# Modulation sections 3 to 6 weighted on VectorE and computed later in the V pass

## The reference, cut to what matters

```python
mod = (_silu(L0_c) @ L0_wmod).reshape(L0_c.shape[0], 6, 1, -1)
sa, ca, ga, sb, cb, gb = (mod[:, 0], mod[:, 1], mod[:, 2], mod[:, 3], mod[:, 4], mod[:, 5])
ga = (2 * (ga >= 0) - 1) * jnp.maximum(jnp.abs(ga), 0.25)
gb = (2 * (gb >= 0) - 1) * jnp.maximum(jnp.abs(gb), 0.25)
h = _layernorm(x, axis=-1) * (1 + ca) + sa
x = x + ga * _L0_attn_ref(h, L0_attn_W_K, L0_attn_W_Q, L0_attn_W_V, L0_attn_W_O)
h = _layernorm(x, axis=-1) * (1 + cb) + sb
x = x + gb * _L0_ffn_ref(h, ...)
```

## Time and profile before

| | us |
|---|---|
| median of 3 runs | 2128.99 (2128.67 to 2129.42) |
| profiled execution, its own time | 2128.4 |
| its span (first to last instruction) | 2126.6 |
| TensorE busy | 2077.6 (98%) |
| VectorE busy | 1352.4 (64%) |
| ScalarE busy | 1029.5 (48%) |
| GpSimd busy | 712.6 (34%) |

### The profile page before, as it was taken

The page is one execution under the profiler, slowest core; times in us unless marked ns, Lnnn a source line. Parts: engine busy times, 40 slices in busy tenths (PEclk is TensorE's granted clock), DMA queues, the critical chain, the costliest instruction groups (busy, mean ns, idle before and its releaser), DMA issues. The chain is left out here.

```text
span 2126.6 us, 36789 instructions
## 1 busy us (share of the span) xinstructions
PE 2077.6 (98%) x12049; PEld 1811.6 (85%) x12049; DVE 1352.4 (64%) x3065; ACT 1029.5 (48%) x1947; POOL 712.6 (34%) x539
## 2 busy tenths in 40 slices
PE   7999899999999999999999999999998999999898
PEld 5778698999999999999999999999997888788687
DVE  7422366675766756656667565565654778799865
ACT  4322355555555545555555555555553333688511
POOL 3310143261442524524336000000026444588300
PEclk9999999999999999999999999999998999999999
DMA  7666312212122121221221201201034666101121
GB/s 266 199 208 188 122 50 63 74 53 77 42 76 67 57 62 42 77 67 57 62 62 57 68 23 52 62 22 52 25 111 145 221 222 231 60 31 40 55 69 60
DMA packets 171419, 189.99 MB, mean 89 GB/s; under 512 B 13395, under 2 KB 119123, under 8 KB 171219
## 3 DMA queue, kind: packets, MB, share of 16 engines
q1 hardware_dynamic: 169043, 184.89, 27.8%
q10 hardware_dynamic: 2304, 4.20, 0.5%
HBM read 121.53 MB, written 67.50 MB: 89 GB/s over the span
## 5 line engine op out<-in xcount | busy, mean ns | idle before, releaser
L1056 ACT ACTIVATE pT_hi<-ps_t 128x512 fp32r<-128x512 f32 (+3 forms) x640 | 304.2, 535 | 250.3 <-PE ps_t L994 248.2
L1137 DVE TENSOR_TENSOR pT_lo<-ps_t,pT_hi 128x512 fp32r<-128x512 f32 (+3 forms) x640 | 356.1, 604 | 62.8 <-ACT pT_hi L1056 62.3
L1064 ACT ACTIVATE probs<-probs,rmin 128x128 f32<-128x128 f32 (+15 forms) x256 | 309.2, 1209 | 161.5 <-DVE rmin L1128 161.0
L193 PE MATMUL ps_z<-pT_lo,v_hi 128*128 128x256 f32 (+1 forms) x1152 | 325.7, 283 | 0.0
L194 PE MATMUL ps_z<-pT_hi,v_lo 128*128 128x256 f32 (+1 forms) x1152 | 325.4, 282 | 0.0
L192 PE MATMUL ps_z<-pT_hi,v_hi 128*128 128x256 f32 (+1 forms) x1152 | 318.4, 276 | 0.3 <-DVE pT_lo L1137 0.3
L994 PE MATMUL ps_t<-ident,probs 128*128 128x128 f32 x2176 | 285.5, 274 | 2.8 <-ACT probs L1064 2.8
L994 PEld LDWEIGHTS ps_t<-ident,probs 128*128 128x128 f32 x2176 | 246.2, 141 | 11.8 <-ACT probs L1064 3.1
L192 PE MATMUL ps_s<-kT_hi,qT_hi 128*128 128x512 f32 (+3 forms) x640 | 248.3, 388 | 1.3 <-DVE qT_lo L1104 1.1
L194 PE MATMUL ps_s<-kT_hi,qT_lo 128*128 128x512 f32 (+3 forms) x640 | 233.4, 365 | 0.0
L193 PE MATMUL ps_s<-kT_lo,qT_hi 128*128 128x512 f32 (+3 forms) x640 | 232.7, 364 | 0.0
(11 more groups left out here) (148 smaller groups left out, 4113.8 us busy)
## 6 DMA issues: line engine op xcount, KB each, us to landing
scratch_v<-p_vo_hi SPq DMA_DIRECT2D x64, 256.0 KB, 2.6
scratch_v<-p_vo_lo SPq DMA_DIRECT2D x64, 256.0 KB, 3.3
v_hi<-scratch_v SPq DMA_DIRECT2D x64, 256.0 KB, 3.4
v_lo<-scratch_v SPq DMA_DIRECT2D x64, 256.0 KB, 3.7
scratch_zT<-z SPq DMA_DIRECT2D x256, 64.0 KB, 1.7
w_raw<-in_w_qkv SPq DMA_DIRECT2D x16, 512.0 KB, 3.7
o_z<-scratch_zT SPq DMA_DIRECT2D x16, 512.0 KB, 6.0
o_scales<-scratch_recips SPq DMA_DIRECT2D x16, 512.0 KB, 7.3
```

Of the source, the lines that this page charges most:

```text
L193: nc.tensor.matmul(dst, stat[0], mov[1], start=False, stop=False)
L1056: nc.scalar.activation(pT[0][:, slot, i % 2, 0:w], ps_t[:, (chunks_before(i) + u) % T_BANKS, 0:w], ACT.Copy).then_inc(t_hi, 1)
L1064: nc.scalar.activation(probs[:, i % 2, 0:w], probs[:, i % 2, 0:w], ACT.Exp, bias=rmin[:, i % 2:i % 2 + 1], scale=-1.0, accum_out=sums[:, i ...
L1137: nc.vector.tensor_tensor(pT[1][:, slot, i % 2, 0:w], ps_t[:, (chunks_before(i) + u) % T_BANKS, 0:w], pT[0][:, slot, i % 2, 0:w].bitcast(F ...
```

## The change

For sections 2 to 5, VectorE now multiplies each of the four chunks of `w_mod` by its 128 values of `silu(c)`, one per partition, and adds the four up in a buffer of 128 x 512 (`summed`, which is the second half of `absr`): one `tensor_scalar` and three `scalar_tensor_tensor` per section (`add_chunk`, the letter K). TensorE then adds over the partitions with one fp32 matmul against `ones`, in place of four. Sections 0 and 1 stay as they were.

The four sections are moved: on TensorE from before V4, V8, V12 and V14 to before V20, V27, V34 and V41. The uses G2 to G5 move behind X20, X27, X34 and X41 on VectorE. On SyncE's queue the loads of sections 2 to 5 move from in front of O0, O0, O4 and O8 to in front of O4, O10, O18 and O25. A load into a half of `wm` now waits for the last K that read it.

```diff
+    summed = absr[:, 1, :]
...
+    part_step = sem("part_step")
...
-    PE_FIRST = """M0 M1 T0.0 T0.1 T0.2 T0.3 V0 V1 T1.0 T1.1 T1.2 T1.3 V2 V3 M2 V4 V5 T2.0 T2.1 T2.2 T2.3 V6 V7 M3 V8 V9
-        T3.0 T3.1 T3.2 T3.3 V10 V11 M4 V12 V13 M5 V14 V15"""
+    PE_FIRST = """M0 M1 T0.0 T0.1 T0.2 T0.3 V0 V1 T1.0 T1.1 T1.2 T1.3 V2 V3 V4 V5 T2.0 T2.1 T2.2 T2.3 V6 V7 V8 V9 T3.0
...
-    V_FIRST = NT
+    V_FIRST = 44
...
-                if s >= 2:
+                if 2 <= s < 4:
                     sp.wait_ge(mod_ready, s - 1)
+                elif s >= 4:
+                    sp.wait_ge(part_step, DC * (s - 3))
...
-            if n == V_FIRST + 6:
-                load("v3")
...
+        def add_chunk(s, c):
+
+            chunk, scale = wm[:, s % 2, c, :], c_silu[:, c:c + 1]
+            if c == 0:
+                dve.wait_ge(wm_loaded[s], 16)
+                dve.wait_ge(mod_used, s)
+                ins = nc.vector.tensor_scalar(summed, chunk, scale, None, ALU.mult)
+            else:
+                dve.wait_ge(part_step, DC * (s - 2) + c)
+                ins = nc.vector.scalar_tensor_tensor(out=summed, in0=chunk, scalar=scale, in1=summed,
+                                                     op0=ALU.mult, op1=ALU.add)
+            ins.then_inc(part_step, 1)
...
             if s >= 2:
                 pe.wait_ge(mod_used, s - 1)
-            pe.wait_ge(wm_loaded[s], 16)
-            for c in range(DC):
-                last = nc.tensor.matmul(ps_mod[:, s % 2, :], c_wide[:, c, :], wm[:, s % 2, c, :],
-                                        start=(c == 0), stop=(c == DC - 1))
+                pe.wait_ge(part_step, DC * (s - 1))
+                last = nc.tensor.matmul(ps_mod[:, s % 2, :], ones[:, :], summed, start=True, stop=True)
+            else:
+                pe.wait_ge(wm_loaded[s], 16)
+                for c in range(DC):
+                    last = nc.tensor.matmul(ps_mod[:, s % 2, :], c_wide[:, c, :], wm[:, s % 2, c, :],
+                                            start=(c == 0), stop=(c == DC - 1))
             last.then_inc(mod_ready, 1)
```

More of the change, by code:

```diff
@@ L398, in prologue @@
     rows_kept = {2: gate_a, 5: gate_b}
-    PE_FIRST = """M0 M1 T0.0 T0.1 T0.2 T0.3 V0 V1 T1.0 T1.1 T1.2 T1.3 V2 V3 M2 V4 V5 T2.0 T2.1 T2.2 T2.3 V6 V7 M3 V8 V9
-        T3.0 T3.1 T3.2 T3.3 V10 V11 M4 V12 V13 M5 V14 V15"""
[L405 to L408, removed]
+    PE_FIRST = """M0 M1 T0.0 T0.1 T0.2 T0.3 V0 V1 T1.0 T1.1 T1.2 T1.3 V2 V3 V4 V5 T2.0 T2.1 T2.2 T2.3 V6 V7 V8 V9 T3.0
+        T3.1 T3.2 T3.3 V10 V11 V12 V13 V14 V15 V16 V17 V18 V19 M2 V20 V21 V22 V23 V24 V25 V26 M3 V27 V28 V29 V30 V31
+        V32 V33 M4 V34 V35 V36 V37 V38 V39 V40 M5 V41 V42 V43"""
+    ACT_FIRST = """D0 H0 H1 H2 H3 A0.0 A0.1 A0.2 D1 A0.3 Y0 Y1 A1.0 A1.1 A1.2 D2 A1.3 Y2 Y3 Y4 D3 Y5 A2.0 A2.1 A2.2
+        A2.3 Y6 Y7 Y8 Y9 A3.0 A3.1 A3.2 A3.3 Y10 Y11 Y12 Y13 Y14 Y15 Y16 Y17 Y18 Y19 Y20 Y21 Y22 Y23 Y24 Y25 Y26 Y27
+        Y28 Y29 Y30 Y31 Y32 Y33 Y34 Y35 Y36 Y37 Y38 Y39 Y40 Y41 Y42 Y43"""
+    DVE_FIRST = """S0 G0 N0 G1 S1 L0.0 L0.1 L0.2 L0.3 N1 X0 X1 S2 L1.0 L1.1 X2 N2 X3 S3 X4 X5 L2.0 L2.1 N3 X6 X7 X8 X9
+        L3.0 L3.1 X10 X11 X12 X13 X14 K2.0 X15 K2.1 X16 K2.2 X17 K2.3 X18 X19 X20 G2 X21 K3.0 X22 K3.1 X23 K3.2 X24
+        K3.3 X25 X26 X27 G3 X28 K4.0 X29 K4.1 X30 K4.2 X31 K4.3 X32 X33 X34 G4 X35 K5.0 X36 K5.1 X37 K5.2 X38 K5.3 X39
+        X40 X41 G5 X42 X43"""
     POOL_FIRST = """I0 I1 I2 I3 L1.2 L1.3 J1.0 J1.1 J1.2 J1.3 L2.2 L2.3 L3.2 L3.3 WK WQ"""
-    SP_FIRST = """Rc Rm0 Rx0 Rm1 Rv0 Rx1 Rx2 Rx3 Rm2 Rm3 Rv1 O0 O1 O2 O3 Rm4 O4 O5 Rv2 Rw O6 O7 Rm5 O8 O9 O10 O11 O12 O13
-        O14 O15"""
-    V_FIRST = NT
+    SP_FIRST = """Rc Rm0 Rx0 Rm1 Rv0 Rx1 Rx2 Rx3 Rv1 O0 O1 O2 O3 Rm2 O4 O5 Rv2 Rw O6 O7 O8 O9 Rm3 O10 O11 O12 O13 O14
+        O15 O16 O17 Rm4 O18 O19 O20 O21 Rv3 O22 O23 O24 Rm5 O25 O26 O27 O28 O29 O30 O31 O32 O33 O34 O35 O36 O37 O38
+        O39 O40 O41 O42 O43"""
+    V_FIRST = 44
     def entries(text):
@@ L633, in _ @@
         for what, arg in entries(DVE_FIRST):
-            {"S": statistics, "G": use_section, "N": normalise, "L": low, "X": value_lo}[what](*numbers(arg))
+            {"S": statistics, "G": use_section, "N": normalise, "L": low, "X": value_lo, "K": add_chunk}[what](*numbers(arg))
         for n in range(V_FIRST, NV):
```

## The result

The changed kernel takes 2130.57 us (median of 22 runs, 2128.45 to 2132.86), the kernel before on the same chip 2128.21 (22 runs). The ratio is 1.0015, with a 95% interval from 1.0009 to 1.0021: slower by 2.4 us by the medians and 3.2 by the ratio, some 0.15%, and outside the predicted range of 2122.1 to 2127.9. The forecast was a gain of 4.1.

What follows compares the result with a forecast made beforehand. TensorE bounds the V pass after V14; before, VectorE, ScalarE and stores run close behind. Terms: 10.3 + 1.9 - 6.5 (new waits) - 1.6 = 4.1 us less, from 2128.99 to 2124.9; range 2122.1 to 2127.9.

Steps and rivals of the forecast that it cites:

- TensorE's work, 10.3 less: Modulation matmuls of four sections: 13.7 us before, 3.4 after, so 10.3 us less on TensorE.
- V5 2.4 late by X3: Before V5, TensorE waits 2.4 us for X3, which stands behind N2 on VectorE.
- the old wait before V6 gone: Before V6, X4 now ends in time, so the earlier wait of 1.9 us disappears.
- V8 1.7 late: Before V8, TensorE waits 1.7 us, since N3 ends at 55.0 and X6 at 55.6.
- V9 1.0 and V12 1.9: Waits of 1.0 us before V9 and 1.9 before V12, with stores O5 and O7 landing late.
- The clock stays up: In TensorE's new gaps before V steps, the sum counted no loss from a lower clock.
- The rival with 0.07: TensorE's clock falls in the new gaps, 2.4 us a step; falls at V5, V8 and V12 give 2132.1; chance 0.07.
- The late loads, 1.6: Loads of sections 4 and 5 behind O17 and O24 make X late and cost 1.6 us.
- The upper bound of 2.6: Both new loads cost 2.6 us if each costs the 1.3 seen at V's last load.
- The jam rival (0.12): Loads behind O17, O21 and O24 overfill the queue by 2.1 us; gain 1.3, time 2127.7; chance 0.12.
- The ring order: On the DMA queue, a load issued behind a store should not delay it; waits 4.6, gain about 6 us.
- K free, VectorE's room: Sixteen K fit into VectorE's 2.06 us of idleness before an X, even at 1.52 each; no cost.

Runs made afterwards that it cites:

- Kernel 8: Changed kernel with the loads of sections 2 and 3 back at their places before the first stores; 2126.9 us, ratio 0.9995.
- kernel 14: Kernel 12 with two matmuls that nobody reads before V5 and one before V8; 2120.41 us, ratio 0.9964.
- kernel 13: Changed kernel with two matmuls that nobody reads before V5 and four before V8; 2130.5 us, ratio 1.0012.
- kernel 3: Changed kernel without VectorE's sixteen K; TensorE's single matmul reads a block of x in place of `summed`; 2130.49 us, ratio 1.0012.
- kernel 6: Changed kernel with the loads of sections 4 and 5 in 256 KB pieces, one behind each of O15 to O18 and O24 to O27; 2125.91 us, ratio 0.9988.
- Kernel 1: Changed kernel without the loads of sections 4 and 5, whose K read what lies in the buffer; 2127.47 us, ratio 0.9998.
- kernel 5: Kernel before with one more 1 MB load that nobody needs, behind O17; 2130.54 us, ratio 1.0009.
- kernel 4: Kernel before with two more 1 MB loads that nobody needs, behind O17 and O24; 2134.5 us, ratio 1.0031.
- kernel 12: Changed kernel with sections 2 and 3 loaded early, sections 4 and 5 and V's last load in pieces, section 5's behind O26 to O29; 2119.62 us, ratio 0.9959.
- Kernel 11: Changed kernel with the loads of sections 2 and 3 before the first stores and those of 4 and 5 in pieces; 2123.35 us, ratio 0.9979.
- kernel 7: Changed kernel, but sections 2 and 3 on four matmuls before V5 and V8, 4 and 5 by K before V18 and V26, loads as before; 2123.1 us.
- kernel 9: Kernel before with V's last load cut into four 256 KB pieces behind O21 to O24; 2126.22 us, ratio 0.9993.
- kernel 2: Changed kernel with two matmuls that nobody reads before V5 and two before V8; 2130.9 us, ratio 1.0015.
- kernel 10: Kernel 7 with V's last load in pieces as well; 2123.58 us, ratio 0.9972.

## Why the prediction was wrong, point by point

- **TensorE's work, 10.3 less: right.** Eight records of 590 ns, 0.88 a section.
- **V5 2.4 late by X3, the old wait before V6 gone: right.** 2.19 by the row, 2.5 with the modelled end.
- **V8 1.7 late: the mechanism right, the size not.** The wait is 2.33 by its row and 2.6 by the steps. The text put section 2's load into the queue and let it hold up O5. It had already held up O3, the store right ahead of it, and O3 releases Y5, which stands before A2 and so before N3, X6 and V8. That is the first failed step, a store that the chain left out. Kernel 8 removed it: Y5 waits 0.39, and V2 to V14 takes 42.63, 0.5 better than forecast.
- **V9 1.0 and V12 1.9: wrong, by their size.** Neither wait is in the trace; together with the small delays from V9 to V14 they are 0.6 by the steps. They were to come from O5 and O7 landing late. O5 did take 7.0, O7 only 3.9, and V6 to V8 being later, there was time for them; where V8 came earlier (kernels 8 and 14), a wait of 0.8 stood before V12.
- **The clock stays up: wrong.** It fell at V5 (step and T2 6.15 in place of 4.41) and at V8 (4.45 in place of 2.75). The rival with 0.07 named the place, and its 2.4 a step was 1.7. Its reasoning from there, that each fall comes off the gain, failed: kernels 13 and 14.
- So the first part reads: V4 and V5 2.8, V8 2.6, clock 3.4, the rest 0.6; 9.4 over bare steps, or 9.0 on the forecast's base, where 6.5 was put. These entries don't add up to what each repair gives: where the clock held at V5 and O3 was late (kernels 3 and 6), the wait before V8 was 3.7 to 3.8 in place of 2.33. Most of the clock's 3.4 and of V8's wait is the same time.
- **The late loads, 1.6: wrong, and the larger failure.** The second part is 136.40 + 3.4 + 4.8. Kernel 1 gives 4.2 of the 4.8 back. This is the second failed step, the price of a load among the steady stores. The forecast took one load's hiccup and counted it as partly hidden behind 0.86 of modulation (its three terms make 1.5, it took 1.6); alone a load costs 2.3 (kernel 5), and the second one 3.7 (kernel 4). The upper bound of 2.6 was itself built from that one hiccup. The jam rival (0.12) had it that loads close together cost more, with a price of 2.1 on top that gives 3.7 in all: still too small. Its reason, more bytes than the DMA engines can move in that time, fails: kernels 6 and 12 move the same bytes there without the loss.
- **The ring order.** The Trainium skill ("DMA: Bandwidth & Descriptors", section "Queues, rings and completion order") says that each DMA engine takes descriptors in ring order. That a load behind a store leaves it alone is what the prediction concluded from this, and not what the section says. Rows of before spoke against the conclusion, and the runs agree with the rows: O3's second store took 5.2 with the load right behind it and 3.1 without.
- **K free, VectorE's room: right** (kernel 3), though K took up to 1.85.
- **The sum.** -4.1, +2.5 and +3.2 give +1.6; the V pass measured +1.65. Kernel 11, the same arithmetic with both queue faults taken out, gives 2123.35, or 4.5 less than before. That this is near the forecast's 4.1 is in part luck, since its V pass is 5.4 shorter.

What is left: the medians say +2.4 where the V pass says +1.65. In the profiled executions, the time that is neither V2 to V63 nor before V2 is 1906.5 to 1906.7 for before and kernels 4, 5, 7 and 9, and from 1905.0 to 1909.1 for the eleven others. The stages behind the pass are not edited in any of them, but the traces show three things that vary. In the output projection of the eleven TensorE waits once behind the stage's start, some 14 us after its first matmul, for 0.4 to 2.4 us; in the other five it waits 0.1 at most there. In the changed kernel:

```profile
1649.22 0.50 PE L192 MATMUL o_pso<-hT_hi,o_zhi 128*128 128x512 f32 x1 [1.25 <-DVE o_zlo L1375]
```

This can make up the missing 0.75. The loads of `o_z` that this low part is made from took 7.2 us to land there and 5.5 before; why is open. The gate and up stage lasts 170.9 at a mean granted clock of 0.99 in eight of the sixteen profiled executions and 172.4 at 0.97 to 0.98 in the other eight, and kernels of both groups are among either. The attention is from 1402.5 to 1404.6. So one profiled execution can lie over 3 us from another outside the V pass, with no edit there.

## What to carry to other kernels

Work taken off the busiest engine is worth what the waits left in its place allow, so walk the chain of buffers (here store, Y, X, V step) for each place where work is taken out. A transfer moved into a steady stream must be priced by its burst: the store just ahead of it is held up as well, whoever waits for that store is hit, and pieces of the stream's own size, one per step, made it free here. One observed hiccup with slack around it was too low a price: 1.5 for V's own load by kernel 9, against 2.3 and 3.7 for the ones added.

## What the runs showed of the hardware

- A 1 MB load in one piece beside steady stores of 256 KB, in the changed kernel: the store right ahead 5.0 to 5.4 instead of 3.1 to 3.3, the two behind 5.9 to 7.5; beside loads of 256 KB in kernel 6 the stores took 2.8 to 4.6. In kernel 12 the DMA share was 0.90 from 84 to 120 us without a stall.
- The granted clock fell to the lower level behind an idle gap of 2.17 to 2.19 us at V5 in the changed kernel and kernels 1, 11 and 12, and did not behind 2.18 to 2.20 in kernels 3, 6 and 8. At V8 it fell behind gaps from 2.12 to 3.79 (changed kernel, kernels 1, 2, 3, 6) and not behind 1.90, 1.36, 1.35, 1.08 or 0.37 (kernels 8, 12, 11, 14, 13). The same gap of 2.2 can go either way.
- A `scalar_tensor_tensor` of 128 x 512 in fp32 on VectorE: 0.74 us alone, 1.76 to 1.85 at 84.64, 87.55 and 136.79 us, where GpSimd split V's weights; there each started within 0.1 us of, or behind, an operation of line 505 on GpSimd (1.30). The K at 90.14 started 0.15 ahead of one: it kept 0.74, and GpSimd's took 1.75.
- A 256 KB store with no load near it took 4.8 and 5.5 us in kernel 10 where an instruction fetch fell on the same DMA engines, and 3.2 in the median between the two fetches.
